# Four target rows in a chunk fetched by index instead of seven, the rest read in order and merged, in two graph attention layers

## The reference

```python
def _transformer_conv(x, src, tgt, edge_attr, Wq, bq, Wk, bk, Wv, bv, We, Wskip, bskip):
    q = (x @ Wq + bq).reshape(N, HEADS, HEAD_DIM)        # HEADS 2, HEAD_DIM 128
    k = (x @ Wk + bk).reshape(N, HEADS, HEAD_DIM)
    v = (x @ Wv + bv).reshape(N, HEADS, HEAD_DIM)
    e = (edge_attr @ We).reshape(E, HEADS, HEAD_DIM)
    alpha = (q[tgt] * (k[src] + e)).sum(-1) / jnp.sqrt(HEAD_DIM)
    a = softmax of alpha over the edges with the same target
    out = jax.ops.segment_sum((v[src] + e) * a[..., None], tgt, num_segments=N)
    return out.mean(axis=1) + x @ Wskip + bskip

x = _layer_norm(x, ln_in_g, ln_in_b)
for l in range(3):
    h = jax.nn.elu(_transformer_conv(x, src, tgt, ...))
    x = _layer_norm(x + h, ln_g[l], ln_b[l])
```

## Time and profile before

| | |
|---|---|
| median of 3 runs | 7995.07 us (7988.37 to 8000.68) |
| profiled execution, first to last instruction | 8002.8 us |
| mean granted TensorE clock in it | 0.822 |
| busy: PE, DVE, ACT, POOL | 5159.0 (64%), 6149.1 (77%), 4810.4 (60%), 4947.2 (62%) us |
| POOL's first gather of layer 1, 2, 3 | 1706.7, 2826.9, 3953.8 us |

### The profile page before, as it was taken

How to read it: one execution, slowest core, us unless ns; L and a number is a source line. 1 busy time by engine, 2 the same in 40 slices (tenths; PEclk the granted TensorE clock), 3 DMA queues, 4 the chain that set the end, 5 groups by cost and what they waited for, 6 DMA issues and landing times. The chain is left out here.

```text
span 8002.8 us, 134106 instructions
## 1 busy us (share of the span) xinstructions
PE 5159.0 (64%) x27083; PEld 3725.0 (47%) x27083; DVE 6149.1 (77%) x29318; ACT 4810.4 (60%) x13748; POOL 4947.2 (62%) x4939
## 2 busy tenths in 40 slices
PE   5013333338888768888577777765995777677671
PEld 2012222226666546666355555544554555555551
DVE  9816777748888758888578888885775868888886
ACT  0005888847777747777466666663554656666663
POOL 7776777737777467777375555515764445555553
PEclk8555555559999879999789998987998988888995
DMA  3334655524444334444243333434656843333331
GB/s 97 101 104 98 137 129 127 128 77 151 158 153 161 129 100 157 156 155 155 90 127 131 131 131 131 132 111 138 204 190 220 281 137 109 111 114 104 115 114 33
DMA packets 493460, 1065.71 MB, mean 133 GB/s; under 512 B 230701, under 2 KB 235896, under 8 KB 492658
## 3 DMA queue, kind: packets, MB, share of 16 engines
q1 hardware_dynamic: 341362, 775.06, 29.5%
q0 software_dynamic: 151424, 284.20, 13.4%
HBM read 559.18 MB, written 500.53 MB: 132 GB/s over the span
## 5 line engine op out<-in xcount | busy, mean ns | idle before, releaser
L1656 POOL DMA_INDIRECT xs<-tab,rec x1176 | 1169.1, 994 | 671.1 <-DVE cA L1801 302.9
L1658 POOL DMA_INDIRECT xd<-tab,rec x1176 | 1156.8, 984 | 358.7 <-issue 352.9
L1742 ACT ACTIVATE z<-p_a 128x512 f32<-128x512 f32 x1176 | 697.7, 593 | 558.9 <-PE p_a L1594 551.1
L1736 ACT ACTIVATE st<-xs,cb 128x128 f32<-128x128 f32 x2352 | 804.8, 392 | 201.2 <-DVEq L1850 201.1
L1594 PE MATMUL p_a<-ident,st 128*128 128x128 f32 x2352 | 510.3, 301 | 474.4 <-DVE st L1812 470.2
L1812 DVE SCALAR_TENSOR_TENSOR st<-st,cg 128x128 f32<-128x128 f32 x2352 | 723.5, 348 | 78.6 <-DVE norm L709 52.3
L1687 PE MATMUL p_a<-w_all,xt 128*128 128x256 f32 x2352 | 755.8, 405 | 10.7 <-ACT xt L1727 10.2
L1690 PE MATMUL p_y<-w_all,xt 128*128 128x258 f32 x2352 | 762.2, 407 | 0.6 <-ACT xt L1727 0.5
L2469 POOL DMA_INDIRECT xs<-res,rec x392 | 421.0, 1074 | 508.4 <-PE p_t L2490 319.0
L1801 DVE CUSTOM_DVE_ANT_0 junk<-p_y,xs 128x129 f32<-128x129 f32 x2352 | 582.9, 285 | 115.3 <-PE p_y L1690 113.0
L1594 PEld LDWEIGHTS p_a<-ident,st 128*128 128x128 f32 x2352 | 289.3, 148 | 815.8 <-DVE st L1812 752.9
(11 more groups left out here) (745 smaller groups left out, 16634.0 us busy)
## 6 DMA issues: line engine op xcount, KB each, us to landing
states<-st SPq DMA_DIRECT2D x168, 910.0 KB
own<-tab SPq DMA_DIRECT2D x168, 448.0 KB
tab<-o SPq DMA_DIRECT2D x168, 448.0 KB
runs<-run SPq DMA_DIRECT2D x112, 448.0 KB, 2.8
tab<-out SPq DMA_DIRECT2D x112, 448.0 KB
x<-tab SPq DMA_DIRECT2D x112, 448.0 KB
angles<-st SPq DMA_DIRECT2D x56, 532.0 KB, 2.8
xsrc<-got SPq DMA_DIRECT2D x56, 448.0 KB
```

Source lines behind the costliest of these rows:

```text
L1656: pool.indirect_dma_start(xs[:, i, j, 0:D], None, table, bass.IndirectOffsetOnAxis(ap=rec[:, i, SRC, j : j + 1], axis=0)).then_inc(got_in[ ...
L1658: pool.indirect_dma_start(xd[:, i, j, :], None, table, bass.IndirectOffsetOnAxis(ap=rec[:, i, PLACE, j : j + 1], axis=0)).then_inc(got_in[ ...
L1736: ins = act.activation(state_of(r, j)[:, h, :], xs[:, c.slot(UB), j, 0:D], ACT.Copy, scale=co.b[:, c.slot(2), h, j : j + 1])
L1742: act.activation(z[:, c.slot(RING), j, :], p_a[two(c, j)][:], ACT.Copy).then_inc(st_copied, 1)
```

## The change

In layers 1 and 2 (not in the third) the target rows of columns 0, 2 and 4 of a chunk are no longer gathered. SP loads the rows that stand at these slots in order, with one DMA of 128 x 3 rows of 512 bytes for chunk c+5, behind a wait on `turned`. Columns 1, 3, 5 and 6 are gathered as before. VectorE then puts the row of column 1, 3, 5 over that of column 0, 2, 4 wherever SAME of the later column says that both have one target (`fill`, one predicated copy of 128 x 3 x 128 values for chunk c+3, at the beginning of j = 3 of chunk c's turn, behind waits for the chunk's 11 gathers and for the load). TensorE waits for that (`xd_filled`) instead of the gathers. VectorE's program gets one lead chunk more. In the third layer `own_rows` is empty: `GOT` is 16 x 14, as the 32 x 7 before, and nothing else changes there but that lead chunk, which issues nothing.

```diff
--- before.py
+++ after.py
@@ -1583,6 +1583,11 @@
         recf = rec[:].bitcast(F32)
         scale = float(D) ** -0.5
         STORE = 7 if last else 4
+        own_rows = () if last else (0, 2, 4)
+        targets = [j for j in range(J) if j not in own_rows]
+        GOT = 16 * (J + len(targets))
+        xd_in = [sem(f"xd_in{u}") for u in range(UB)]
+        xd_filled = sem("xd_filled")
         halves = lambda t: t.rearrange("p (h x) -> p h x", h=H)
         state_of = lambda r, j: halves(st[:, r, j, 0 : 2 * D])
         flat = lambda t: t.rearrange("p j d -> p (j d)")
@@ -1622,6 +1627,10 @@
                         wait(sp, resid, c.count(1, 1 - UB), passed)
                         sp.dma_start(rec[:, c.slot(UB)].rearrange("p f j -> p (f j)"),
                                      k.meta[:, c.n].rearrange("p f j -> p (f j)")).then_inc(rec_in[c.slot(UB)], 16)
+                        if own_rows:
+                            wait(sp, turned, c.count(J, (1 - UB) * J), passed)
+                            sp.dma_start(xd[:, c.slot(UB), 0:6:2, :],
+                                         table.rearrange("(p b j) d -> p b j d", p=P, j=J)[:, c.n, 0:6:2, :]).then_inc(xd_in[c.slot(UB)], 16)
                     c = Chunk(k, t, u, 2)
                     if c.there:
                         wait(sp, turned, c.count(J, 1 + J), passed)
@@ -1655,8 +1664,9 @@
                         wait(pool, scored, c.count(J, j + 1 - 3 * J), passed)
                         pool.indirect_dma_start(xs[:, i, j, 0:D], None, table,
                                                 bass.IndirectOffsetOnAxis(ap=rec[:, i, SRC, j : j + 1], axis=0)).then_inc(got_in[i], 16)
-                        pool.indirect_dma_start(xd[:, i, j, :], None, table,
-                                                bass.IndirectOffsetOnAxis(ap=rec[:, i, PLACE, j : j + 1], axis=0)).then_inc(got_in[i], 16)
+                        if j in targets:
+                            pool.indirect_dma_start(xd[:, i, j, :], None, table,
+                                                    bass.IndirectOffsetOnAxis(ap=rec[:, i, PLACE, j : j + 1], axis=0)).then_inc(got_in[i], 16)
 
                 walk(k, pool, one, 0, 0)
 
@@ -1667,7 +1677,10 @@
                     if not (c.there or own_c.there):
                         return
                     if i == 0 and c.there:
-                        pe.wait_ge(got_in[c.slot(UB)], (c.use(UB) + 1) * 32 * J)
+                        if own_rows:
+                            pe.wait_ge(xd_filled, c.count(1, 1))
+                        else:
+                            pe.wait_ge(got_in[c.slot(UB)], (c.use(UB) + 1) * GOT)
                     if own_i == 0 and own_c.there:
                         pe.wait_ge(own_in[own_c.slot(2)], (own_c.use(2) + 1) * 16)
                     wait(pe, copied, c.count(J, i - 1))
@@ -1803,6 +1816,14 @@
                                                        co.A[:, c.slot(2), h, 1 + j : 2 + j])
                     ins.then_inc(scored, 1)
 
+                def fill(c):
+
+                    i = c.slot(UB)
+                    wait(dve, got_in[i], (c.use(UB) + 1) * GOT, passed)
+                    wait(dve, xd_in[i], (c.use(UB) + 1) * 16, passed)
+                    same = rec[:, i, SAME, 1:6:2].unsqueeze(2).to_broadcast([P, 3, D])
+                    dve.copy_predicated(xd[:, i, 0:6:2, :], same, xd[:, i, 1:6:2, :]).then_inc(xd_filled, 1)
+
                 def add_state(c, j):
                     dve.wait_ge(weighted, c.count(J, j + 1))
                     state.land()
@@ -1819,10 +1840,11 @@
 
                 def one(t, u):
                     ahead, mid, c, c1, c2, c3, c4, c5 = [Chunk(k, t, u, lag) for lag in (SCORE, SHARE, 0, -1, -2, -3, -4, -5)]
+                    early = Chunk(k, t, u, SCORE + 1)
                     if ahead.there:
                         i = ahead.slot(UB)
                         wgt.at(ahead)
-                        dve.wait_ge(got_in[i], (ahead.use(UB) + 1) * 32 * J)
+                        dve.wait_ge(got_in[i], (ahead.use(UB) + 1) * GOT)
                         wait(dve, weighted, ahead.count(J, (1 - UB) * J))
                         wgt(dve.tensor_copy(xs[:, i, :, 0:1], field(ahead, WGT).unsqueeze(2)))
                         wgt.end()
@@ -1840,6 +1862,8 @@
                             co.level(n, coef, dve, mid.slot(2), field(mid, SAME))
 
                     for j in range(J):
+                        if own_rows and early.there and j == 3:
+                            fill(early)
                         if mid.there and j == co.ASK:
                             coef.land()
                             dve.nop().then_inc(exp_in, 1)
@@ -1910,7 +1934,7 @@
                         state.land()
                         state.end()
 
-                walk(k, dve, one, SCORE, 5 if last else 3)
+                walk(k, dve, one, SCORE + 1, 5 if last else 3)
 
 
         room, used = xd[:].rearrange("p r j d -> p (r j d)"), [0]
```

## The result

The changed kernel takes 8023.07 us (median of 14 runs, 8008.63 to 8034.07), the one before 7996.87 us (14 runs, 7988.37 to 8006.93): ratio 1.003, 95% interval 1.0022 to 1.0038, 0.3% slower. The profiled execution of the changed kernel is the shortest of its 14 (8008.63 us, span 8006.9); that of before is longer than its median. So their spans differ by 4 us only, where the medians differ by 26; what follows compares stretches (each between the same two chunks), not spans.

The account below looks back on a forecast made before the run. The prediction took POOL's gathers to limit layers 1 and 2, VectorE 0.3 to 0.4 us a chunk behind. Relief -36, ramp -20 and fill +81 made +25 us on 7995, 8020 us, range 7972 to 8062.

Parts of the forecast that it names:

- case D: The prediction's own case: 8020 us, from 8000 to 8045 by a fill of 0.7 to 1.05 us; chance 0.52.
- POOL stops being the limit, VectorE takes over: Layers 1 and 2: POOL drops from 18.1 to 14.2 us a chunk, VectorE limits at 17.2 to 17.8.
- Relief at full pace, -36: Layers 1 and 2 at full pace: VectorE's waits at TensorE go, -36 us; bounds 31 and 60.
- The ramp, -20: Start of layers 1 and 2: chunks land sooner with 11 gathers, 10 us a layer, -20 us; bounds 4 and 15 a layer.
- The fill, +81: VectorE, layers 1 and 2: 100 unhidden fills of 0.49 us copy plus 0.32 us waits, +81 us; 0.49 to 1.27 each.
- layer 3: 0: Third attention layer, where the work stays the same: no change in time, 0 us.
- Sum: Whole kernel: -36 - 20 + 81 = +25 us, 8020 us on the median, 0.3% slower.
- A: Rival: the waits in front of the fill on VectorE cost nothing, 7988 us, or 7978 with the longer ramp; chance 0.25.
- B: Rival: POOL's gathers hold up the fill on VectorE, 8045 us, or 8056 if fully blocked; chance 0.18.
- C: Rival: the fill waits for rows or gathers, a new wait replacing the old, 8120 us; chance 0.05.
- TensorE's wait: TensorE's new wait for the fill at j = 6, three columns after it: cost 0.
- SP's load: SP's one extra DMA a chunk, issued five chunks ahead and used three ahead: cost 0; a late load was a rival.

Follow-up runs that it names:

- no_fill: The changed kernel without the fill, TensorE waiting for gathers and load itself: 7908.86 us, ratio 0.989 to the kernel before.
- fill_twice: The changed kernel with a second, equal copy at j = 4 behind a wait for the first: 8046.21 us, ratio 1.0058 to the kernel before.
- fill_on_14: All 14 gathers a chunk kept, nothing loaded in order, the fill put on top: 8051.49 us, ratio 1.0066 to the kernel before.
- after_again: The changed kernel itself measured and traced once more: 8030.23 us, ratio 1.0037 to the kernel before.
- head_shift_13: The changed kernel with the fill at the head of a turn and 13 empty instructions before VectorE's walk in each layer: 7972.24 us, ratio 0.997.

## Why the prediction was right, and where

8020 us was forecast and 8023 measured, within the range, and case D is the one that happened: POOL off the path, the fill bare on VectorE, a little slower in the end. That the sum came within 3 us is luck. The relief was put at 56 us and the fill at 81; by medians no_fill is 89 us under the kernel before, and the changed kernel 114 to 121 over no_fill. Both terms were 33 to 40 us too small and offset each other.

- *POOL stops being the limit, VectorE takes over*: as put; POOL's idle rows, the wait at TensorE and fill_twice show it. The two stand close: with 14 gathers and the fill (fill_on_14) VectorE still waits for POOL in the first chunks of each stretch.
- *Relief at full pace, -36*: 54 by no_fill. What the term names came true: the waits at TensorE fell from 36 us to 1. The step that failed is to count only them. VectorE's busy time fell too, from 15.78 and 15.66 us a chunk to 15.59, 13 us in all, and the idle time at layer 2's turns from 17.5 to 11.9. The upper bound of 60 held it.
- *The ramp, -20*: with the fill, as it was forecast, 29 (14 and 15 a layer), at the upper bound of 15; without it 42. Left out of the sum were the 9 us between chunk 54 and the next layer, which also got shorter.
- *The fill, +81*: against no_fill 43.4 and 42.6 us at full pace and 7 in each ramp, 100 in all. The copy was sized right (0.49 forecast, 0.49 measured), though from a misread row: the 0.57 us of the earlier trace rows is the median of four shapes, and the one at 128x384 took 0.585, as the fill does (0.589). The waits were sized right too (0.32 net; 0.27). What no term held is the idle time at the loop's turns, 3.8 to 5.7 us where no_fill has 2.5 to 3.3, some 0.12 a chunk, and 8 to 10 us in layer 3, where it stands inside the loop's body and not at the turns. The prediction had "layer 3: 0".
- *Sum*: -54 - 42 - 11 + 100 + 8 = +1 from these traces; the medians say +26. The execution profiled before was at least 6 us over its median and the changed one 14 under. after_again's trace is 14 us longer than the changed kernel's first one, with 9 of it in the three stretches and 4 behind chunk 54 of layer 3; it is spread out, and what causes it isn't shown.
- *A* falls: 0.30 us of idle time and more in front of each fill inside the loop, and 0.19 in the mean in fill_on_14, with one wait less. *B* falls: 112 fills took 0.585 to 0.648 us, so no gather held one up by even 0.07; 103 of them began while a gather was running, and of these the longest took 0.617. The Trainium skill ("SBUF — State Buffer", Who interferes with whom) would have VectorE blocked where POOL came first; this case's fills disagree. For POOL's side the gathers agree with it: 71 of the 539 in layer 1 took over 1.1 us, up to 1.84, and 63 of these ran mostly beside L1906 or L1915 and 6 beside a fill. *C* falls: at full pace no wait of a fill on a DMA shows in layer 1 or 2.
- *TensorE's wait* on the fill cost nothing at full pace, as forecast: no wait of VectorE behind it shows. No wait of a fill on SP's load shows there either. Neither was changed by itself.

## What to carry to other kernels

Before an engine is relieved, ask how far behind it the next one stands: here 0.55 us a chunk of 3.9 was to be had, and the instruction that bought it cost 0.88. An instruction that is added to the limiting engine should go in front of a place where that engine steps through waits anyway: the same copy cost 0.88 us a chunk bare and 0.33 in the shadow of the root's wait, and that turned 0.3% slower into 0.4% faster. And where a few tenths of a per cent are at stake, shift the code more than once without changing the work, to see how much of a difference comes from that.

## What was not expected of the hardware

In all of these kernels VectorE idles at each turn of the attention loop. In the trace of the changed kernel its sequencer's last record in front of that idle time is the loop's branch, at 3306.02 us, and the next one comes at 3310.31. Over these kernels the piece is 2.5 to 5.7 us long, 6.1 twice in the kernel before. It is much the same for one kernel and layer in most cases and changes when empty instructions are put in front of the loop (layer 3 of the kernel before: 2.5 to 2.7, with 13 of them 4.7 to 5.2). Short pieces at fixed chunks inside the loop change too. That empty instructions in front change both is shown; that it is through the place of the loop is likely and not shown, why isn't shown either, and no rule for a good place came out of three amounts (0, 5 and 13). Whole kernels moved by 5 to 18 us when the empty instructions were added, in either direction, and not all of that lies in the loops of layers 1 to 3 (head_shift_13).
